# Edge convolution: the twelfth tile of a chunk, picked by matmuls or gathered by GpSimd

## What is computed

```python
h = jnp.maximum(_layernorm(x, axis=-1), 0.0)
x_i = h[dst]
x_j = h[src]
feat = jnp.concatenate([x_i, x_j - x_i], axis=-1)
m = jnp.maximum(feat @ W1 + b1, 0.0) @ W2 + b2
out = jax.ops.segment_max(m, dst, num_segments=x.shape[0])
x = x + jnp.where(jnp.isneginf(out), 0.0, out)
```

## Time and profile before

| | |
|---|---|
| median of three runs | 5022.33 us (5005.23 to 5023.61) |
| the profiled execution's own time | 5046.15 us |
| its span, first to last instruction | 5044.3 us |
| mean granted TensorE clock | 0.794 of full speed |
| instructions | 58734 |
| TensorE matmuls busy | 3240.3 us, of it L676 2318.6 us |
| GpSimd busy | 3109.6 us, of it L393 2785.5 us |
| VectorE busy | 2493.6 us |
| ScalarE busy | 1025.4 us |
| HBM traffic | 89 GB/s over the span |

### The profile page before, as it was taken

The page is one execution under the profiler, slowest core; times in us unless marked ns, Lnnn a source line. Parts: engine busy times, 40 slices in busy tenths (PEclk is TensorE's granted clock), DMA queues, the critical chain, the costliest instruction groups (busy, mean ns, idle before and its releaser), DMA issues.

```text
span 5044.3 us, 58734 instructions
## 1 busy us (share of the span) xinstructions
PE 3240.3 (64%) x14598; PEld 1876.2 (37%) x14861; DVE 2493.6 (49%) x8363; ACT 1025.4 (20%) x4057; POOL 3109.6 (62%) x3186
## 2 busy tenths in 40 slices
PE   2100137777777777777777777777777777777970
PEld 2100014444444444444444444444444444444540
DVE  4100115555555555555555555555555555556871
ACT  4300212212122121221212222122221212212320
POOL 5777756666666666666666666666666666664017
PEclk8555558888888888888888888888888888888985
DMA  7866312222222222222222222222222222222222
GB/s 274 315 229 227 115 32 73 67 73 70 70 73 67 73 70 70 70 70 73 70 70 69 70 73 69 70 70 69 73 67 73 70 70 72 69 72 71 80 77 56
DMA packets 239614, 452.86 MB, mean 90 GB/s; under 512 B 94781, under 2 KB 95402, under 8 KB 238738
## 3 DMA queue, kind: packets, MB, share of 16 engines
q1 hardware_dynamic: 97663, 225.75, 14.2%
q0 software_dynamic: 103216, 117.29, 11.1%
q10 hardware_dynamic: 38362, 105.62, 5.4%
HBM read 230.84 MB, written 217.71 MB: 89 GB/s over the span
## 4 chain that ended last, share of the span: by engine, by line
another core or an unknown queue 41%; issue 28%; DVE 10%; ACT 9%; PE 7%; POOL 2%; ACTq 2%; DMA 1%; DVEq 1%; POOLq 0%; SPq 0%
ACT dst_all L549 5%; DVE state L911 4%; PE ps_g L676 4%; DVE a_fill L885 3%; PE ps_m L696 2%; POOL a_rows L456 2%; ACT zt L560 2%; ACTq L567 1%; DMA shared<-in_x_dram 1%; DVE rows L897 1%; ACT zt L474 1%; ACT keep L531 1%; PE ps_t L687 0%; ACT shared L501 0%
## 5 line engine op out<-in xcount | busy, mean ns | idle before, releaser
L393 POOL DMA_INDIRECT rows<-b_table,src_idx x2865 | 2785.5, 972 | 1523.6 <-issue 805.7
L676 PE MATMUL ps_g<-shared,dst_all 128*128 128x512 bf16 x9468 | 2318.6, 400 | 174.3 <-issue 170.5
L676 PEld LDWEIGHTS ps_g<-shared,dst_all 128*128 128x128 bf16 x9731 | 1011.1, 105 | 1329.5 <-issue 417.3
L696 PE MATMUL ps_m<-w_diag,zt 128*128 128x128 f32 x3126 | 707.8, 411 | 920.2 <-ACT zt L560 917.8
L696 PEld LDWEIGHTS ps_m<-w_diag,zt 128*128 128x128 f32 x3126 | 638.2, 308 | 1056.3 <-ACT zt L560 1049.8
L911 DVE SCALAR_TENSOR_TENSOR state<-state,keep,ps_m 128x64 f32<-128x64 f32 x3125 | 862.3, 276 | 202.5 <-PE ps_m L696 166.7
L885 DVE SCALAR_TENSOR_TENSOR a_fill<-a_fill,keep 128x64 f32<-128x64 f32 x3144 | 879.6, 280 | 53.1 <-DVE a_fill L885 41.6
L935 DVE TENSOR_TENSOR dst_all<-ps_s,page_keys 128x1664 bf16<-128x1664 f32 x132 | 249.6, 1891 | 816.0 <-remote 795.1
L935 DVE TENSOR_TENSOR dst_all<-ps_x,page_keys 128x1664 bf16<-128x1664 f32 x132 | 249.6, 1891 | 794.7 <-remote 774.7
L560 ACT ACTIVATE zt<-ps_t 128x512 f32<-128x512 f32 (+1 forms) x521 | 226.4, 486 | 1517.9 <-remote 1511.6
L549 ACT ACTIVATE dst_all<-ps_g,dst_all 128x64 f32<-128x64 f32 x2096 | 458.1, 347 | 33.2 <-DVE rows L944 33.2
(11 more groups left out here) (116 smaller groups left out, 877.0 us busy)
## 6 DMA issues: line engine op xcount, KB each, us to landing
a_edges<-state SPq DMA_DIRECT2D x80, 1250.0 KB
a_fill<-a_edges SPq DMA_DIRECT2D x260, 384.0 KB
states<-state ACTq DMA_DIRECT2D x260, 384.0 KB
rows<-b_table,src_idx POOLq DMA_INDIRECT x2865
src_idx<-in_src_dram SPq DMA_DIRECT2D x234, 6.0 KB
shared<-in_x_dram SPq DMA_DIRECT2D x5, 625.0 KB
b_table<-shared ACTq DMA_DIRECT2D x5, 625.0 KB
a_table<-a_rows SPq DMA_DIRECT2D x1, 3125.0 KB
```

The lines of the kernel that those rows point to most:

```text
L393: nc.gpsimd.indirect_dma_start(out=rows[:, slot, t * C:(t + 1) * C], out_offset=None, in_=b_table, in_offset=at(src_idx[:, slot, :], t)).t ...
L676: last = nc.tensor.matmul(ps_g[:, half, :], key_is[:, half, g, :], table[:, g, t, :], start=(g, t) == (0, 0), stop=g == PAGES - 1)
L696: last = nc.tensor.matmul(ps_m[:, g, a * C:(a + m) * C], zt[0:m * C, g, a * C:a * C + P], w2_pair[0:m * C, 0:m * C], start=True, stop=True)
```

## The change

The twelfth tile is gathered by GpSimd as the eleven others are. `GATHERED` goes, `gather_chunk` issues 12 indirect DMAs a chunk, and all waits on `gathered` count 12. Gone are the page table and its loads, the picks, keys, masks and octets on TensorE, ScalarE and VectorE with their semaphores, and the waits of SP on them. `xs` is a tensor of its own and no longer a view of the table's memory. The ring, the other steps and their order on each engine stay. The diff, cut:

```diff
-    KEYS_AHEAD, MATCH_AHEAD, PICK_AHEAD, CHOOSE_AHEAD = 5, 4, 3, 2
-    FREE = 2
-    GATHERED = CHUNK - 1
     FILL_AHEAD = 3
...
-        shared = sb("shared", [P, PAGES * PARTS * OCTET * C // 2])
-        xs = shared[:, 0:NJ * C].rearrange("p (j c) -> p j c", c=C)
+        xs = sb("xs", [P, NJ, C])
...
-            for g in range(PAGES):
-                load_page(g)
...
-            sp.wait_ge(page_part, PAGES * PARTS)
-            sp.wait_ge(bits_split, KEYS_AHEAD)
...
-                    sp.wait_ge(gathered[k], (i + 1) * 16 * GATHERED)
+                    sp.wait_ge(gathered[k], (i + 1) * 16 * CHUNK)
...
-            sp.wait_ge(picked, CHUNKS + PICK_AHEAD + FREE)
...
-            def gather_chunk(slot, tiles=GATHERED, done=None):
+            def gather_chunk(slot, tiles=CHUNK, done=None):
...
-                    spread_keys(c + KEYS_AHEAD, k + KEYS_AHEAD)
...
-                if tiles == CHUNK:
-                    mask(c + CHOOSE_AHEAD, k + CHOOSE_AHEAD)
...
-                if whole:
-                    pick(c + PICK_AHEAD, k + PICK_AHEAD, range(PAGES_FIRST))
...
-                if whole:
-                    turn_keys(c + KEYS_AHEAD, k + KEYS_AHEAD)
-                    pick(c + PICK_AHEAD, k + PICK_AHEAD, range(PAGES_FIRST, PAGES))
...
-                dve.wait_ge(gathered[k], (full + 1) * 16 * GATHERED)
+                dve.wait_ge(gathered[k], (full + 1) * 16 * CHUNK)
...
-                dve.wait_ge(chosen, c + 1 + FREE)
...
-                    prepare_picks(c, k, i)
...
-                        if t == CHUNK - 2:
-                            choose(c + CHOOSE_AHEAD, (k + CHOOSE_AHEAD) % RING)
```

More of the change, by code:

```diff
@@ L293, in clear @@
                              zero_row).then_inc(zeros_stored[half], 16)
[L295 to L311, removed]
             for half in range(2):
@@ L568, in step @@
                               ).then_inc(state_stored[k % 2], 16)
-            for g in range(PAGES):
-                page_loads = g // 2 + 1
-                if g == PAGES - 1:
-                    page_loads += PARTS * (1 + (N % OCTET > 0)) - 1
-                act.wait_ge(page_loaded[g % 2], 16 * page_loads)
-                if g == 0:
-                    act.wait_ge(b_stored, 16 * PIECES)
-                for t in range(PARTS):
-                    if t >= 1:
-                        act.wait_ge(page_left, 1 + g * (PARTS - 1) + t)
-                    nc.scalar.activation(table[:, g, t, :], page[:, g % 2, :], ACT.Copy).then_inc(page_part, 1)
-            act.wait_ge(page_part, PAGES * PARTS)
-            for t in range(1, PARTS):
-                quarter = slice(t * QUARTER, (t + 1) * QUARTER)
-                nc.scalar.activation(table[quarter, PAGES - 1, 0, :], table[quarter, PAGES - 1, t, :],
-                                     ACT.Copy).then_inc(table_ready, 1)
             act.wait_ge(same_ready, 1)
@@ L592, in _ @@
                 act.sem_inc(state_stored[half], 16)
-            act.sem_inc(octet_masked, FREE)
-            act.sem_inc(keys_spread, FREE)
-            for c in range(-KEYS_AHEAD, 0):
-                spread_keys(c + KEYS_AHEAD, c + KEYS_AHEAD)
-            for c in range(CHOOSE_AHEAD):
-                mask(c, c)
             act.wait_ge(a_scattered, 16 * NJ)
@@ L660, in _ @@
             w2_pair = w2_diag[:, :, :].rearrange("p h n -> p (h n)")
-            def turn_keys(c, k):
-                pe.wait_ge(keys_spread, c + 1 + FREE)
-                pe.wait_ge(keys_matched, c - 1 + FREE)
-                nc.tensor.matmul(ps_k[k % 2], ones_h[:, :], key_diag[:, k % 2, :], start=True, stop=True).then_inc(keys_turned, 1)
-            def pick(c, k, pages):
-                half = k % 2
-                if pages[0] == 0:
-                    pe.wait_ge(keys_matched, c + 1 + FREE)
-                    pe.wait_ge(octet_masked, c - 1 + FREE)
-                for g in pages:
-                    for t in range(PARTS if g < PAGES - 1 else 1):
-                        last = nc.tensor.matmul(ps_g[:, half, :], key_is[:, half, g, :], table[:, g, t, :],
-                                                start=(g, t) == (0, 0), stop=g == PAGES - 1)
-                if pages[-1] == PAGES - 1:
-                    last.then_inc(picked, 1)
             def step(c, k, tiles=CHUNK):
-                whole = tiles == CHUNK
                 for g, n in groups(tiles):
@@ L841, in _ @@
             nc.vector.tensor_tensor(lane_i[:, 1:2], lane[:, 4:5], lane[:, 5:6], ALU.add).then_inc(caps_ready, 1)
-            nc.vector.tensor_copy(ident_h[:, :], ident[:, :])
-            link(nc.vector.tensor_copy(page_keys[:, :], page_i[:, :]))
-            for t in range(1, PARTS):
-                quarter = page_keys[t * QUARTER:(t + 1) * QUARTER, PAGES - 1:PAGES]
-                nc.vector.tensor_scalar(quarter, quarter, -float(t * QUARTER), None, ALU.add)
-            nc.vector.tensor_copy(octets[:, :], rank[:, 0:OCTET]).then_inc(picks_set, 1)
-            for g in range(PAGES):
-                for t in range(PARTS - 1):
-                    dve.wait_ge(page_part, g * PARTS + t + 1)
-                    nc.vector.tensor_tensor(page[:, g % 2, :], page[:, g % 2, :], table[:, g, t, :],
-                                            ALU.subtract).then_inc(page_left, 1)
             for half in range(2):
```

115 lines of the change are left out of this document (3 added, 112 removed).

## The result

The kernel after takes 5173.3 us (median, 5170.73 to 5175.14) beside 5019.2 us for the kernel before (5005.23 to 5023.61). The ratio is 1.031, its 95% interval 1.029 to 1.033: the change makes it 3% slower. Forecast were 4462 us and 11% faster.

The account below looks back on a forecast made before the run. GpSimd and TensorE were taken to hold each other at a full ring; without picks GpSimd alone bounds. Setup 736, loop 3580, last gathers 6.4, tail about 12 and 151.9 behind gave 4486, less 24: 4462 us, range 4380 to 4975.

Parts of the forecast that it names:

- the work of a chunk without GpSimd's: Loop: the other engines' steps take 8.3 us a chunk, far under GpSimd's 15.3 us, so GpSimd bounds the loop.
- the setup: Ahead of the loop: 25 added gathers cost 33 us, the 35.2 us stop goes, and the setup ends at 736 us.
- TensorE's share: Whole kernel after: TensorE's busy share falls to near 25%, from 64% before.
- the low granted clock: Loop: the clock stays low without picks, as while the profiled messages ran; already in the 8.3 us a chunk.
- Part 3, where the gap goes: Loop: without picks, transposes are released well inside a 15.3 us burst, so GpSimd's stop ahead of each chunk vanishes.
- the 2.8 us: Loop: GpSimd's wait for transposes ahead of each chunk, 675.3 us in all, taken as gone; bounds 0 to 2.8 us.
- The 24 us: Whole kernel: taken off the 4486 us span, since before's median lay 24 us under its profiled execution.
- Rival 2: Loop: late hand-overs beside unbroken issue stop GpSimd every second chunk, 16.6 us a chunk, 4968 us; chance 0.09.
- Rival 1: Loop: late release stays behind each burst, which grows 1.275 us; 17.9 us a chunk, 5272 us; chance 0.13.
- the five hand-overs of rival 2: Each chunk: transposes, relu, messages, maxima, relu again; each 1.5 us late or more beside GpSimd would pass 15.3 us.
- the 7 us from which that rival decides: Loop: total hand-over lateness a chunk from which the other engines can't keep up with GpSimd; that rival's chance 0.09.
- 5.7 us from the setup: Setup: TensorE's longest waits for others beside indirect DMAs are 2 to 5.7 us, against 11 us needed to stop GpSimd.

Follow-up runs that it names:

- e1: Kernel after without GpSimd's gathers in the loop, all loads, stores and other engines' steps kept: 3013 us, on the first kind of chip.
- e2: Kernel after with eleven gathers a chunk in the loop instead of twelve, so picks and twelfth gather both gone: 4852 us, first kind of chip.
- g1: Kernel before, with GpSimd waiting ahead of each chunk's eleven gathers until the chunk before has landed: 4595.7 us, second kind of chip.
- g3: Kernel after, with the loop's gathers taking 32 columns of each row instead of 64: 4456.7 us, second kind of chip.
- e4: Kernel after, with GpSimd waiting ahead of each chunk's twelve gathers until the chunk before has landed: 4978.3 us, 0.992 of before, first kind of chip.
- h2: Kernel before, with GpSimd waiting ahead of each chunk's gathers until the chunk before has landed: 5007.4 us, 1.000 of before, first kind of chip.

## Why the prediction was wrong

What was right: the work of a chunk without GpSimd's, 8.3 us forecast, 8.0 to 8.1 measured, but only while GpSimd is quiet; the setup, chunk 26 at 736 forecast, 744.1 measured; the gathers' own cost, 0.970 and 0.966 us; TensorE's share; that the low granted clock isn't the limit (8.06 us a chunk at 0.63 in e1).

What failed is **Part 3, where the gap goes**. I took the 2.8 us as caused by picks that stood between transposes and their news, and the 8.3 us of a chunk as holding beside unbroken gathers. Taking the picks away alone (e2) brought the period only from 16.62 to 15.98 us, where eleven gathers without a gap would take 13.75. And picks alone make no gap: before wasn't profiled on chips B and D, but with g1's start of the loop (663.5) and what follows its end (177.7), its 4077 us leave (4075 - 663.5 - 177.7) / 234 = 13.8 us a chunk, eleven times 1.26. The gap was mostly the lateness of one kind of chip (the picks' share was about 0.6 us), and it went from every chunk to every second one, 111 stops of 4.9 us. Term by term against the forecast span of 4486: start +8, loop 234 x (17.36 - 15.30) = +482, tail 367 instead of 170, +197; together the 687 us to 5173. The 24 us that the forecast took off its span weren't there either: after's median is its span.

**Rival 2** named the mechanism (hand-overs late beside unbroken issue, a stop about every second chunk, some 150 transposes left) and had 0.09. Its size was off: it averaged 15.3 and 17.9 us, and the pace is 12 x 1.447; it gave 4968 us. **Rival 1**, stops behind each burst, isn't what is seen; that its 5272 us came nearer than either is luck. I argued rival 2 down with VectorE's prompt steps in the earlier trace rows. All of those lie in the first 9 us of a burst, and in this kernel a burst never lasts over 14 us; they could not show what happens behind. The rows that could were those of the setup, with up to 7.64 us of waiting beside a long row of indirect DMAs, and I used them as a bound for single hand-overs, five a chunk. VectorE's chain has 24 steps a chunk that wait on its own semaphores, which the five hand-overs of rival 2 leave out; at 1.12 us each, seven of them pass the 7 us from which that rival decides. And a hand-over between engines, which I bounded by 5.7 us from the setup, came up to some 20 us late. The 1.95 us by which ScalarE went on behind a burst in the earlier trace rows (GpSimd itself went on after 2.77 us, not with it as I wrote) may have been a price too: over eleven gathers it is 0.18 us each, and 1.25 + 0.18 = 1.43 is near the floor that the runs showed. That is an estimate in hindsight; no run tests it.

The rule of the Trainium skill (Perfetto Trace Analysis, Optimizing GPSIMD Operations) that I named beside rival 1, to prefer other engines over GpSimd, came out as it says on the first kind of chip, where the change away from TensorE costs 3%. The other rule that I named (the Trainium skill, Perfetto Trace Analysis, Identifying the Most-Contended Engine) I read short: for TensorE that section doesn't go by the busy share of its matmuls but by the share of its weight loads or its FLOPs. The weight loads had 37% and GpSimd 62%, so of these two GpSimd was the engine to relieve, and the change loaded it.

On the second kind, GpSimd alone would have been the bound, as forecast: g3, which moves half the bytes in the loop and is otherwise the kernel after, takes 4457 us, 15.34 us a chunk against the 15.30 of the forecast, with 9 transposes left. That its time is so near 4462 is partly luck: its loop starts 44 us earlier than the forecast has it, which hides the 24 us and the dearer chunk. And before takes 4079 us there, so the change would cost some 9%. That ratio is worked out; after itself wasn't run on such a chip. No kernel here is ahead of before on both kinds: e4 is 0.8% ahead on chip A, and on B and D nothing came under before's 4077.

What stays open: why a gather costs 1.45 us on chips A, C and E and 1.25 us on B and D, and whether that is lasting in a chip, since each was used only once. Open too is why ScalarE's L560 was late within 14 us of a burst, while VectorE's steps in after are mostly prompt for that long. The steps of 1.40 us on VectorE and the independence of rows suggest one piece of work per gather that engines' semaphore updates queue behind. That is argued, not shown; no row has it.

## What to carry to other kernels

A busy engine's gap ahead of each burst shows who waits, not who is to blame: before work is taken away to close it, ask whether anything at all is prompt so late in a burst, and read the same hand-over at several distances from the burst's start. Count an engine's waits for itself as hand-overs. One more gather a chunk costs what the long run shows (here about 1.4 us a chunk), which may be more than the distance at which gathers start (1.25 us). A producer that fills a ring pays for the full ring once more at the end. Making it wait took that tail off in e4 (192 us) without slowing the loop, but gained nothing in h2 and cost 13% in g1 on the other kind of chip: time such a wait, and time both kernels, on more than one chip.

## What the runs showed of the hardware

The same kernel took a fifth less time on some chips than on others: before took 5016, 5049 and 5010 us on three, and 4077 and 4079 us on two, the medians of seven to thirteen runs. On the first kind, beside indirect DMAs issued by GpSimd, many of VectorE's steps that wait for its own semaphores came 0.70 or 1.40 us apart after about 14 us of unbroken issue, instead of 0.19 (43% of them stood over 0.3 us from 14 to 18 us, 78% from 20 to 28 us, 5% in the first 8 us), and a maximum stood up to 27.7 us. Without picks, the long-run pace of gathers was 1.447 to 1.458 us there, with 64 or 128 rows, with or without memsets between them; beside picks it was 1.494 to 1.512 us. On the second kind it was GpSimd's pitch alone, 1.22 us with 64 rows and 1.28 us with half the bytes, and GpSimd never stopped in the loop, but for the wait put into g1.
